# A three-part layer on one core: the last group and its rest in another order on four engines

## The reference

```python
# 1. cross attention over 257 context rows of 192 channels, 16 heads of 64
q = layernorm(x) @ Wq ; k, v = split(context @ Wkv)
x = x + softmax(where(mask, q @ k.T / 8, -inf)) @ v @ Wo + bo
# 2. self attention over the 32 tokens of a batch, 16 heads of 16
q, k, v = split(layernorm(x) @ W_qkv + b_qkv)
x = x + softmax(q @ k.T / 4) @ v @ W_proj + b_proj
# 3. feed forward with a token shift
xr, xk = (mu * x + (1 - mu) * x_prev  for mu in (mu_r, mu_k))
x = x + sigmoid(xr @ W_r.T) * (square(relu(xk @ W_k.T)) @ W_v.T)
```

## Time and profile before

| | us |
|---|---|
| median of three executions | 845.15 |
| the profiled execution | 844.62 |
| its span, first to last instruction | 842.7 |
| PE busy | 799.9 (95%) |
| ACT busy | 604.0 (72%) |
| DVE busy | 600.3 (71%) |
| POOL busy | 415.0 (49%) |

### The profile page before, as it was taken

One profiled execution on the slowest core, in us unless ns is written; L12 is line 12 of the kernel. 1 busy time (PEld: TensorE's weight loads), 2 busy tenths in 40 slices (PEclk: granted clock), 3 DMA queues, 4 the chain that ended last, 5 costly groups with the idle time before them and its releaser, 6 DMA issues.

```text
span 842.7 us, 20502 instructions
## 1 busy us (share of the span) xinstructions
PE 799.9 (95%) x7501; PEld 665.1 (79%) x7501; DVE 600.3 (71%) x1813; ACT 604.0 (72%) x1439; POOL 415.0 (49%) x664
## 2 busy tenths in 40 slices
PE   9999899999999999998999999999999989888885
PEld 8988688876889678895888768896788957777664
DVE  5865857786687956788577866879568783767375
ACT  3998767796678956887678966789568875677422
POOL 1356345663456624763456624566247633475311
PEclk9999999999999999999999999999999999999999
DMA  9311110110101200011101101012000110100000
GB/s 238 131 40 38 50 26 14 39 58 8 30 11 39 63 23 17 16 33 56 26 14 39 48 17 27 14 39 63 17 24 14 29 48 14 26 14 1 27 2 14
DMA packets 49523, 30.53 MB, mean 36 GB/s; under 512 B 22928, under 2 KB 48336, under 8 KB 49424
## 3 DMA queue, kind: packets, MB, share of 16 engines
q1 hardware_dynamic: 48528, 29.12, 12.7%
q10 hardware_dynamic: 896, 0.10, 0.1%
HBM read 26.85 MB, written 2.10 MB: 34 GB/s over the span
## 4 chain that ended last, share of the span: by engine, by line
PE 78%; DVE 14%; ACT 3%; issue 3%; POOL 1%; POOLq 0%; ACTq 0%; DVEq 0%
PE score L807 17%; PE probT L818 6%; PE post L895 6%; PE pre L657 6%; DVE qk_t L1356 4%; DVE qk_l L1352 3%; PE post L904 3%; PE aux L746 3%; PE ac_main L835 3%; PE ac_tail L837 3%; PE ac_main L836 3%; PE ac_tail L841 3%; PE ac_main L840 2%; PE post L875 2%; PE post L881 2%
## 5 line engine op out<-in xcount | busy, mean ns | idle before, releaser
L431 POOL TENSOR_TENSOR prT_l<-prT,prT_h 128x512 fp32r<-128x512 f32 x128 | 166.0, 1298 | 197.3 <-ACT prT_h L1128 196.7
L565 POOL TENSOR_SCALAR pr<-pr,rsum,poison 128x257 f32<-128x257 f32 x256 | 146.3, 582 | 131.2 <-DVE rsum L1380 131.1
L1109 ACT ACTIVATE pr<-sm,nmx 128x257 f32<-128x257 f32 x256 | 129.6, 507 | 62.1 <-DVE nmx L1374 61.1
L1374 DVE CUSTOM_DVE_ANT_0 sm<-score,mbias 128x257 f32<-128x257 f32 x256 | 106.8, 420 | 80.3 <-PE score L807 65.5
L807 PE MATMUL score<-cT_h,qk_h 128*128 128x258 f32 x256 | 90.0, 351 | 6.7 <-DVE qk_t L1356 5.0
L1128 ACT ACTIVATE prT_h<-prT 128x512 fp32r<-128x512 f32 x128 | 80.6, 631 | 20.0 <-PE ac_tail L841 18.7
L818 PE MATMUL probT<-ident,pr 128*128 128x128 f32 x512 | 79.2, 277 | 0.7 <-ACT prT L1117 0.7
L1117 ACT ACTIVATE prT<-probT 128x512 f32<-128x512 f32 x128 | 75.6, 591 | 2.9 <-PE probT L818 1.7
L807 PE MATMUL score<-cT_h,qk_t 128*128 128x258 f32 x256 | 72.8, 284 | 0.0
L1387 DVE TENSOR_TENSOR act_<-ac_tail,act_low 64x256 f32<-64x256 f32 x128 | 52.8, 412 | 28.1 <-ACT act_low L1141 26.8
L807 PE MATMUL score<-cT_h,qk_l 128*128 128x258 f32 x256 | 72.5, 283 | 0.0
(11 more groups left out here) (319 smaller groups left out, 2181.5 us busy)
## 6 DMA issues: line engine op xcount, KB each, us to landing
cx_in<-in_ctx_dram SPq DMA_DIRECT2D x64, 192.0 KB, 2.5
cx_in<-in_ctx_dram SPq DMA_DIRECT2D x64, 64.0 KB, 2.3
xn<-in_x_dram SPq DMA_DIRECT2D x8, 256.0 KB, 3.0
xb<-in_x_dram SPq DMA_DIRECT2D x8, 256.0 KB, 3.0
out_dram<-yo SPq DMA_DIRECT2D x7, 256.0 KB, 2.2
wq<-in_L_xattn_Wq_dram SPq DMA_DIRECT2D x2, 512.0 KB, 6.0
wo<-in_L_xattn_Wo_dram SPq DMA_DIRECT2D x1, 1024.0 KB, 8.0
wqkv<-in_L_attn_W_qkv_dram SPq DMA_DIRECT2D x1, 768.0 KB, 8.9
```

The source lines that it names most:

```text
L431: eng.tensor_tensor(prT_l[:, :, cut], prT[:, :, cut], prT_h[:, :, cut], ALU.subtract).then_inc(prob_lower, 1)
L565: last = pool.tensor_scalar(p, p, rsum[:, j % 2, t:t + 1], poison[:, 0:1], ALU.mult, ALU.mult)
L1109: act.activation(pr[j % 2][:, t, :], sm[:, t % 2, :], ACT.Exp, bias=nmx[:, j % 2, t:t + 1], scale=-1.0, accum_out=ssum[:, j % 2, t:t + 1]) ...
L1374: dve.tensor_tensor_reduce(sm[:, t % 2, :], score[t % 2][:, 0:NK], mbias[:], DH ** -0.5, BIG, ALU.add, ALU.min, nmx[:, j % 2, t:t + 1]).th ...
```

## The change

The four tables of the last group, `PE_LAST`, `ACT_LAST`, `DVE_LAST` and `POOL_LAST`, are written anew. They hold the same jobs, and every job has the same instructions and the same waits; only `Z17` and `Z18` are gone, so there are 17 fillers instead of 19. The tables of the groups before are untouched. Cut to a few lines, with the end of PE's table and of DVE's:

```diff
 PE_LAST = (
...
-    "FR FK P1:6 LT.0 FV S3:7 AC:6 P0:7 OT0.0 OT1.0 P1:7 LT.1 WO.0 AC:7 OT0.1 T2.0 OT1.1 QT.0 KT.0 WO.1 Z0 SC.0 VR.0 Z1 Z2 "
...
+    "S2:7 FK AC:5 S3:7 P1:6 FV P0:7 AC:6 OT0.0 P1:7 LT.1 OT1.0 AC:7 WO.0 OT0.1 OT1.1 Z0 WO.1 T2.0 QT.0 KT.0 Z1 T2.1 QT.1 "
+    "KT.1 Z2 SC.0 Z3 Z4 Z5 VR.0 Z6 SC.1 Z7 VR.1 PT.0 PV.0 Z8 T4.0 PT.1 PJ.0 PV.1 Z9 T4.1 PJ.1 Z10 T3.0 Z11 Z12 Z13 Z14 "
...
 DVE_LAST = (
...
-    "C8.0 PJ.1 C0.1 C1.1 C2.1 C9.0 C3.1 C4.1 C5.1 C6.1 C7.1 C8.1 C9.1 M1.0 M1.1 FR.0 FR.1 SG.0 FV.0 SG.1 FV.1").split()
+    "C8.0 C9.0 PJ.1 C0.1 C1.1 C2.1 C3.1 C4.1 C5.1 C6.1 C7.1 C8.1 C9.1 M1.0 M1.1 FR.0 FR.1 SG.0 SG.1 FV.0 FV.1").split()
...
-FILL = tuple(f"Z{n}" for n in range(19))
+FILL = tuple(f"Z{n}" for n in range(17))
```

More of the change, by code:

```diff
@@ L73 @@
 PE_LAST = (
[5 rows of a table removed]
-    "T3.0 Z17 T3.1 FR.0 FK.0 FR.1 FK.1 Z18 FV.0 FV.1").split()
[5 rows of a table added]
+    "T3.1 FR.0 FK.0 FR.1 Z15 FK.1 Z16 FV.0 FV.1").split()
 ACT_FIRST = (
@@ L92 @@
 ACT_LAST = (
[5 rows of a table removed]
-    "T4.1 T3.0 M0.0 T3.1 M0.1 FK.0 EZ.0 FK.1 EZ.1").split()
[5 rows of a table added]
+    "T3.0 M0.0 T3.1 M0.1 FK.0 EZ.0 FK.1 EZ.1").split()
 DVE_FIRST = (
@@ L125 @@
 POOL_LAST = (
-    "N0:0 CT:1 N1:0 CT:2 XB L0:0 N0:1 CT:3 L1:0 CT:4 L0:1 N1:1 N0:2 L1:1 N1:2 X1 CT:5 N0:3 L0:2 N1:3 W0 L1:2 W1 L0:3 N0:4 "
-    "CT:6 N1:4 LX L1:3 N0:5 CT:7 N1:5 L0:4 L1:4 N0:6 L0:5 L1:5 N1:6 KA L0:6 L1:6 N0:7 YO N1:7 L0:7 CT:0 L1:7 XB.0 X1.0 "
+    "CT:1 XB N0:0 CT:2 N1:0 L0:0 LX N0:1 N1:1 CT:3 L1:0 N0:2 CT:4 N1:2 L0:1 L1:1 X1 CT:5 N0:3 L0:2 L1:2 N1:3 CT:6 W0 W1 "
+    "L0:3 N0:4 N1:4 CT:7 L1:3 N0:5 N1:5 L0:4 L1:4 N0:6 N1:6 L0:5 L1:5 CT:0 KA N0:7 L0:6 L1:6 N1:7 YO L0:7 L1:7 XB.0 X1.0 "
     "X1.1 W.0 W.1 KA.0 KA.1 YO.0 YO.1").split()
```

## The result

Four executions of the changed kernel took 833.27, 834.02, 835.41 and 836.75 us, median 834.71; the kernel before, beside them, 845.01. The ratio is 0.988, 95% interval 0.9856 to 0.9904: 10.3 us sooner. Forecast were 838.0 us and a range of 835.0 to 842.5. So the sign was right, the gain was larger than forecast, and the median lies 0.3 us under the range. The profiled executions, at mean granted clocks of 1.000 before and 0.995 after, differ by 9.2 us only.

A forecast was written before the change was run, and what follows sets the result against it. It took TensorE's work plus waits to bound the last group, a four-engine chain the rest. Gains of 6.1 (waits) and 3.8 (WO.0) less 2.6 (rest) gave 7.3 us off 845.15: 838.0 us, range 835.0 to 842.5.

The forecast's parts named there:

- (a): Last group: reordering cuts TensorE's waits from 10.1 us to 4.0, a gain of 6.1 us.
- the walk: Last group, job by job with traced durations, each starting once engine and inputs are free: eight small waits, 2.7 us.
- 84.4 us of work up to AC:7: Last group from OT0: 98.28 less 10.1 of waits and 3.8 for WO.0, before adding 4.0 of waits left.
- (b): End of the last group: WO.0 moved behind AC:7 lets AC:7 start 3.8 us sooner.
- (c): The rest, from AC:7's start to the last yo: 52.8 us against 50.2, 2.6 us more.
- SM.1 to PJ.1 ... 6.2 in both: In the rest, SM.1 to PJ.1 goes through the same eight hand-overs, 6.2 us before and after.
- The halves meet on VectorE: In the rest, the halves lose their stagger: WO.1's copy to SM.1 takes 18.0 us against 16.1, 1.9 more.
- (d): Other queues: SP's later loads land just before CT:5 and CT:7 need them; 0 to 0.5 us if not.
- (e): VectorE sigmoid adds meeting GpSimd subtractions: 0.8 us a collision, none taken beyond 1.3 us of (a), 0 to 3 collisions for the range.
- Rival 3: Slower, because TensorE's clock falls in the rest, with 2.0 us idle between VR.1 and PT.0; chance 0.05.
- my own signs of being wrong: AC:7 starting after 784, 55 us or more from it to the last yo, or clock below 1.00 before FV.1.
- Rivals 1 and 2: Last group: waits move onto VectorE, 7 us stay, 841.8 us, chance 0.20; or all 10.1 return, 843.9 us, chance 0.07.

The follow-up runs named there:

- T2 alone: The change with AC:0 put back ahead of S1:2 and S2:2 on TensorE alone, so T2 waits for hn again: 835.24 us, ratio 0.9881.
- FK: The change with product FK of the last group put directly behind FR again, on TensorE alone: 834.9 us, ratio 0.9879.
- early values: The change with values made early, VectorE copying them ahead of KM.1 and behind SM.1, and 25 fillers for 17: 831.46 us, ratio 0.9842.

## Why the prediction was right or wrong

**(a) Waits in the group: right in mechanism, the size failed.** "A walk misses small delays at hand-overs, so I take 4.0" is the step. The waits that were left measure 1.4 us, not 4.0, and under the walk's own 2.7. S2:5, S3:5, T4 and T3 lie where the walk had them (0.19, 0.53, 0.13 and 0.31 us for 0.35, 0.6, 0.45 and 0.3), and T2 waits no more, as it said. So nothing had to be put on top of the walk, and the 4.0 was the mistake: 2.6 us of the error. The other 1.2 were in "84.4 us of work up to AC:7", which I had by taking the idle rows from the stage. It took 84.59 - 1.40 = 83.2: a wait hides more than its row, since the product behind it starts without the 0.16 us of overlap with the one ahead and is itself a little longer. The two samples above put this at 0.19 us (T2 alone) and 0.25 (FK); over the nine waits or so that went (8.8 us by their rows) it came to 1.3 us, 0.14 each. The old group with the new rest agrees: with idle time of 9.92 us instead of 1.40 its TensorE is busy 84.41 us for the same jobs, 1.2 more. That all of it is broken overlap is worked out from two samples and not shown for each wait. So (a) gained 10.1 us where I had 6.1. My bounds of 2.7 and 10.1 for what would be left were the second mistake: the lower one was the walk itself, and the outcome lay under it.

**(b) WO.0: 3.6 us, forecast 3.8.** Right within the change; alone it is 6 us slower, which I had not seen, since LT.1 then holds CL:7 up. AC:7 started at 776.68, not 780.5: the 3.8 us of (a).

**(c) The rest.** To the copy of WO.1's sum 15.2 us (15.3 forecast); from there to SM.1 17.95 (18.0), of which KM.1 to SM.1 10.8 (10.8); SM.1 to PJ.1 8.03 (6.2), 6.30 in the runs with the clock up; PJ.1 to the last yo 12.8 (13.3). In sum 53.97 where I had 52.8, and 52.28 where the clock held. "SM.1 to PJ.1 ... 6.2 in both" is thus the second step that failed, by the clock alone. "The halves meet on VectorE" was the cost, and the kernel with early values takes most of it back: 50.85 us, where before it was 50.21.

**(d)** CT:5 and CT:7 do not wait: the loads are covered. **(e)** No sigmoid addition of the last group met a subtraction; 0.29 and 0.27 us, where one had taken 1.07. A longer instruction beside GpSimd's work shows elsewhere: L1450 takes 0.17 us at 804.31 and, beside the normalisation that GpSimd starts at 804.85 (1.05 us), 0.58 at 805.35, in the kernel with early values. In the change no collision was found on the path.

**Rival 3 came true in small.** The clock fell at 808.06, behind VR.1, where I had counted 2.0 us of idle and the row shows 1.25. I gave the case 0.05. The trace of before has no fall while TensorE works, so it shows no price for one. The fall came in three of the four executions, by their mean clocks; in the profiled one it lasted 6.83 us, and it cost 1.7. With that one of my own signs of being wrong was met, a clock below 1.00 before FV.1. I had tied the fall to the order and to the fillers taken out; the kernel before falls as well, in 9 of 28 executions, if less often than the new rest's 18 of 26, and my rows came from one that did not. The two mistakes of size, 3.8 us sooner and 1.2 later in the rest (1.7 for the clock, less 0.5 of slack in (c)), leave 2.6 us in the span. The profiled execution took 2.6 us beyond its span, where that of before took 1.9; no run says why. That the median came as near as 0.3 us to the range is in part luck: the one execution at 1.000 took 833.27, 1.7 us under it.

The stretches at half clock did not cost in step with their length. The one of 6.83 us cost 1.7 us on the path and the one of 20.48 us 5.1, a quarter of the length in both; but two stretches of 3.41 us cost 1.7 (the new group alone) and 1.6 (no filler, behind PJ.1), about half. What counts is what lies on the path: in the change the first 3 us of the stretch, up to PT.1 at 811.07, fall behind VectorE's and GpSimd's work, and then PT.1, PJ.0 and PV.1 take 1.09, 1.92 and 1.08 us for 0.63, 1.03 and 0.65, 1.8 more. For the 20.48 us this is not worked out. What the fillers show is 832.93 us with 26 of them and 835.97 with none, 3.0 us, and a mean clock of 0.997 or less in one execution of four and in all four; by what they hold it is not shown.

**Rivals 1 and 2** fell: VectorE is dense from KM.1 to SM.1, but in the group its density holds up TensorE only at S2:5 and S3:5, 0.7 us together. The range failed on its lower side: it allowed 3.0 us for a better group (its two parts of 1.3 each give 2.6), and 3.8 came.

## What to carry to other kernels

Price a wait of TensorE at its row plus the overlap that it breaks (here 0.14 us on average, 0.2 to 0.25 in the two samples), and give a walk through the queues an error on both sides. Before a long job is moved from in front of another, look at what the other one waits for: the job may be the cover, and moving it alone may cost more than it brings. Where both halves of a split chain meet on one engine, move the work that nobody waits for (here the value copies) into its pauses, and keep the fillers in the same edit (early values took 831.46 us with 25 fillers and 836.75 with none). Before a fall of the clock is put down to a change, look at the mean clocks of all executions of both kernels, not at one profile of each.

## What the runs showed of the hardware

- A granted clock of 0.50 came with idle stretches of TensorE no longer than 1.25 us ahead of it, in a stage of which TensorE was busy 12.57 of 16.16 us. It ran on through 6.83 us in which TensorE was busy for 6.48. Stretches at half clock measured 3.41, 6.83 and 20.48 us, and cost 1.6 to 1.7, 1.7 and 5.1 us of the path.
- In the kernel with only WO.0 moved, the fall came after the idle time. Behind the wait of 3.79 us, AC:7's first products ran at a granted clock of 1.00 for 1.3 us (790.33 to 791.62), and then, with TensorE busy, it was 0.50 for 3.41 us.
- The same program falls in one execution and not in the next: 833.27 us at a mean clock of 1.000, 835.41 at 0.995. Its four executions spread over 3.5 us, the five of the kernel that stays at 0.999 to 1.000 over 0.8. The clock does not order them all: 836.75 us had 0.996.
